# Causal attention: maxima of two heads in the two halves of the array's rows, one burst a step, values two steps behind

## The reference, cut to what matters

```python
Q = (X @ Wq.T + bq).reshape(B, S, H, d_head) * scale
K = (X @ Wk.T + bk).reshape(B, S, H, d_head) * scale
V = (X @ Wv.T + bv).reshape(B, S, H, d_head)
scores = jnp.einsum('bqhd,bkhd->bhqk', Q, K)
causal = jnp.tril(jnp.ones((S, S), bool))
scores = jnp.where(causal[None, None], scores, -jnp.inf)
attn = jax.nn.softmax(scores.astype(jnp.float32), axis=-1).astype(X.dtype)
out = jnp.einsum('bhqk,bkhd->bqhd', attn, V).reshape(B, S, D)
return out @ Wo.T + bo
```

## Time and profile before

| | us |
|---|---|
| median of the runs (3) | 2040.08 |
| lowest, highest | 2039.08, 2040.45 |
| profiled execution, its own time | 2036.14 |
| its span, first to last instruction | 2034.0 |
| TensorE matmuls busy | 1682.5 (83%) |
| VectorE busy | 1383.6 (68%) |
| ScalarE busy | 939.3 (46%) |
| GpSimd busy | 672.0 (33%) |
| mean granted clock of TensorE | 0.923 of 2.4 GHz |

### The profile page before, as it was taken

How to read it: one execution, slowest core, us unless ns; L and a number is a source line. 1 busy time by engine, 2 the same in 40 slices (tenths; PEclk the granted TensorE clock), 3 DMA queues, 4 the chain that set the end, 5 groups by cost and what they waited for, 6 DMA issues and landing times. The chain is left out here.

```text
span 2034.0 us, 35680 instructions
## 1 busy us (share of the span) xinstructions
PE 1682.5 (83%) x10296; PEld 1295.6 (64%) x10296; DVE 1383.6 (68%) x2825; ACT 939.3 (46%) x2201; POOL 672.0 (33%) x850
## 2 busy tenths in 40 slices
PE   2899985709991780799999999996789999979997
PEld 2787774509991560455555555542579999968886
DVE  5688887506665876977777777760467777646776
ACT  0456562304443651066666666664444444433343
POOL 1555530750007824043434334343000000047760
PEclk9799998959995995899999999998899999989999
DMA  6445523723434996333535354422774444466661
GB/s 217 181 141 168 156 47 65 230 91 117 125 113 127 332 355 190 85 105 86 147 85 144 94 129 109 118 68 64 205 216 125 125 126 125 127 212 182 202 181 47
DMA packets 288529, 293.13 MB, mean 144 GB/s; under 512 B 122665, under 2 KB 245034, under 8 KB 286300
## 3 DMA queue, kind: packets, MB, share of 16 engines
q1 hardware_dynamic: 265340, 236.62, 39.6%
q0 software_dynamic: 18432, 50.36, 7.9%
q10 hardware_dynamic: 4608, 4.20, 0.6%
HBM read 144.97 MB, written 141.82 MB: 141 GB/s over the span
## 5 line engine op out<-in xcount | busy, mean ns | idle before, releaser
L1705 ACT ACTIVATE ca_PT<-ca_psS 128x512 f32<-128x512 f32 (+3 forms) x768 | 344.9, 493 | 272.8 <-PE ca_psS L1740 260.4
L1631 DVE TENSOR_REDUCE ca_part<-ca_psM 128x1 f32<-128x512 f32 (+3 forms) x608 | 368.6, 657 | 85.3 <-PE ca_psM L1725 60.5
L1740 PE MATMUL ca_psS<-ca_QS,ca_KS 128*128 128x512 f32 (+3 forms) x768 | 305.7, 408 | 4.2 <-ACT ca_PT L1705 4.1
L1033 POOL DMA_INDIRECT g_y<-ys_scratch,pos x128 | 129.6, 1013 | 441.7 <-POOLq L68 395.0
L1718 PE MATMUL ca_psM<-ca_KS,ca_QS 126*128 126x512 f32 (+3 forms) x768 | 246.5, 364 | 15.6 <-issue 12.8
L1740 PEld LDWEIGHTS ca_psS<-ca_QS,ca_KS 128*128 128x128 f32 x768 | 147.1, 194 | 106.7 <-ACT ca_PT L1705 101.7
L1718 PEld LDWEIGHTS ca_psM<-ca_KS,ca_QS 126*128 126x128 f32 x768 | 141.1, 193 | 37.9 <-DVE ca_part L1631 15.6
L1752 PE MATMUL ca_psO<-ca_PT,ca_VA 128*32 128x512 f32 (+3 forms) x1536 | 160.7, 497 | 1.3 <-POOL ca_PT L1611 1.3
L1609 POOL TENSOR_TENSOR ca_waited<-ca_waited 1x1 f32<-1x1 f32 x128 | 23.4, 183 | 341.7 <-ACT ca_PT L1705 341.7
L626 POOL DMA_INDIRECT xs_scratch<-x_sb,pos x128 | 123.3, 964 | 36.8 <-issue 36.8
L497 PE MATMUL fa_psO<-fa_weighed,ident 128*128 128x256 f32 x512 | 124.0, 398 | 8.1 <-DVE fa_weighed L356 8.0
(11 more groups left out here) (288 smaller groups left out, 4567.2 us busy)
## 6 DMA issues: line engine op xcount, KB each, us to landing
f_xs<-xs_scratch SPq DMA_DIRECT2D x214, 128.0 KB, 2.1
ys_scratch<-f_ys SPq DMA_DIRECT2D x214, 128.0 KB, 1.7
xs_scratch<-fa_blank SPq DMA_DIRECT2D x32, 640.0 KB, 4.1
ca_QS<-qk_scratch SPq DMA_DIRECT2D x32, 512.0 KB, 6.6
ca_KS<-qk_scratch SPq DMA_DIRECT2D x32, 512.0 KB, 8.2
xs_scratch<-fa_blank SPq DMA_DIRECT2D x32, 384.0 KB, 3.4
f_raw<-in_ffn SPq DMA_DIRECT2D x16, 608.0 KB, 4.0
v_scratch<-gp_v_st SPq DMA_DIRECT2D x32, 256.0 KB, 4.5
```

Of the source, the lines that this page charges most:

```text
L1033: pool.indirect_dma_start(dst[:, k, :], None, y_dram, bass.IndirectOffsetOnAxis(pos[:, tile, k:k + 1], 0)).then_inc(got, 16)
L1631: dve.tensor_reduce(dst, psM[(slot * NU + u) % SLOTS][:, 0:nh * w].rearrange("p (h k) -> p h k", h=nh), AX.X, ALU.max)\
L1705: act.activation(PT[:, s % 2, h, off:CHUNK], psS[(GH * s + h) % SLOTS][:, off:CHUNK], ACT.Exp)\
L1740: pe.matmul(psS[tile % SLOTS][:, off:CHUNK], KS[:, slot, h, kt * P:(kt + 1) * P], QS[:, slot, h, c * CHUNK + off:(c + 1) * CHUNK], start=T ...
```

## The change

Six things change in `causal_attention`.

1. The maxima get stacks of their own, `QM` and `KM`: 64 dense rows a head. The first two heads of a group lie in partitions 0 to 63, the other two in 64 to 127. A unit makes its matmuls in pairs, one in each half of the array's rows, into the two banks of a pair (`psM` is now two pairs of banks). The mask is added with two matmuls a unit, which use all rows. VectorE reduces both banks with one instruction. There are 20 units a round and `FIRST` is 8.
2. ORDER becomes "0123uuv": the four scores, then the units, then the values.
3. PT has three slots, and the values are those of two steps before.
4. `psX` goes. The transposes of the output and of the maxima take their turn in the pairs of psM (`place` numbers all users of the pairs in order, with two semaphores, `pair_filled` and `pair_taken`).
5. The transpose of the output of a chunk comes three steps after its last step (`OUT`): in the seventh step for the first chunk, and in the third step of the next round for the second.
6. Two slots instead of three for QS, KS and VA; QM and KM have two of their own, loaded in eight DMAs a round (`pull_pairs`). The last round is written like the others.

```diff
-    SLOTS = 3
+    SLOTS, PAIRS, PTS = 2, GH // 2, 3
...
+        QM, KM = sb("QM", [P, SLOTS, PAIRS, SEQ], F32R), sb("KM", [P, SLOTS, PAIRS, SEQ], F32R)
-        PT = sb("PT", [P, 2, GH, CHUNK])
-        units = [(qt, k0, w, h0, min(CHUNK // w, GH)) for qt in range(POS_TILES)
+        PT = sb("PT", [P, PTS, GH, CHUNK])
+        units = [(qt, k0, w, p0, min(CHUNK // w, PAIRS)) for qt in range(POS_TILES)
                  for k0, w in [(k, min(CHUNK, (qt + 1) * P - k)) for k in range(0, (qt + 1) * P, CHUNK)]
-                 for h0 in range(0, GH, min(CHUNK // w, GH))]
+                 for p0 in range(0, PAIRS, min(CHUNK // w, PAIRS))]
...
-        ORDER = "0u1u2u3uv"
+        ORDER = "0123uuv"
+        OUT = [(s + 3) % NS for s in (max(s for s, (c, _, _) in enumerate(steps) if c == cc) for cc in range(SPAN))]
...
-        psM = [ctx.enter_context(nc.psum_tensor(f"ca_psM{i}", [P, CHUNK], F32)) for i in range(SLOTS)]
-        psS = [ctx.enter_context(nc.psum_tensor(f"ca_psS{i}", [P, CHUNK], F32)) for i in range(SLOTS)]
+        BANKS = 3
+        psM = [ctx.enter_context(nc.psum_tensor(f"ca_psM{i}", [P, 2, CHUNK], F32)) for i in range(2)]
+        psS = [ctx.enter_context(nc.psum_tensor(f"ca_psS{i}", [P, CHUNK], F32)) for i in range(BANKS)]
-        psX = ctx.enter_context(nc.psum_tensor("ca_psX", [P, CHUNK], F32))
...
+            def pull_pairs(n):
+                slot = n % SLOTS
+                if n >= SLOTS:
+                    sp.wait_ge(pair_filled, place["unit", n - SLOTS, NU - 1] + 1)
+                rows = qk_dram[:, :, n, :, :].rearrange("c s (r g h) n -> s g r c (h n)", g=2, h=PAIRS)
+                for g in range(2):
+                    for half in range(2):
+                        part = slice(g * P // 2 + half, (g + 1) * P // 2, 2)
+                        sp.dma_start(QM[part, slot, :, :]...).then_inc(pairs_in[slot], 16)
+                        sp.dma_start(KM[part, slot, :, :]...).then_inc(pairs_in[slot], 16)
...
+            def banks(at):
+                if at >= 2:
+                    pe.wait_ge(pair_taken, at - 1)
+                return psM[at % 2]
-            def unit(n, slot, u):
+            def unit(n, u):
+                pair = banks(place["unit", n, u])
                 for h in range(nh):
-                    ins = pe.matmul(bank[:, h * w:(h + 1) * w], QS[0:STACK, slot, h0 + h, qt * P:(qt + 1) * P],
-                                    KS[0:STACK, slot, h0 + h, k0:k0 + w], start=True, stop=not diag, skip_group_check=True)
+                    for g in range(2):
+                        half = slice(g * P // 2, (g + 1) * P // 2)
+                        ins = pe.matmul(pair[:, g, h * w:(h + 1) * w], QM[half, n % SLOTS, p0 + h, qt * P:(qt + 1) * P],
+                                        KM[half, n % SLOTS, p0 + h, k0:k0 + w], start=True, stop=not diag, skip_group_check=True)
                 if diag:
-                    ins = pe.matmul(bank[:, 0:nh * w]..., ident_b[:, :], mask, start=False, stop=True, ...)
+                    for g in range(2):
+                        ins = pe.matmul(pair[:, g, 0:nh * w]..., ident_b[:, :], mask, start=False, stop=True, ...)
...
                         elif part == "v":
-                            if s:
-                                values(n, slot, s - 1)
+                            if n * NS + s >= PTS - 1:
+                                values(*divmod(n * NS + s - (PTS - 1), NS))
...
-                    if s == last_step[0] + 2:
+                    if s == OUT[1] and n:
+                        transpose_out(n - 1, 1)
+                    if s == OUT[0]:
                         transpose_out(n, 0)
-                    if s == WHOLE - 1:
+                    if s == WHOLE - 1 and n + 1 < ROUNDS:
                         transpose_maxima(n + 1)
-                values(n, slot, NS - 1)
-                transpose_out(n, 1)
```

More of the change, by code:

```diff
@@ L1519, in causal_attention @@
         stack_in = [sem(f"stack_in{i}") for i in range(SLOTS)]
+        pairs_in = [sem(f"pairs_in{i}") for i in range(SLOTS)]
         m_in = [sem(f"m_in{i}") for i in range(SLOTS)]
         ao_stored = [sem("ao_stored0"), sem("ao_stored1")]
[L1522 to L1534, removed]
@@ L1536, in first, with next_place @@
-        def first(n):
-            return isinstance(n, int) and n == 0
+        LOADS, PAIR_LOADS = 5, 8
+        place = {}
+        def next_place(*x):
+            place[x] = len(place)
+        for u in range(NU):
+            next_place("unit", 0, u)
+        next_place("maxima", 0)
+        for u in range(FIRST):
+            next_place("unit", 1, u)
+        for n in range(ROUNDS):
+            for s in range(NS):
+                for u in ahead[s]:
+                    if n + 1 + s // WHOLE < ROUNDS:
+                        next_place("unit", n + 1 + s // WHOLE, u)
+                if s == OUT[1] and n:
+                    next_place("out", n - 1, 1)
+                if s == OUT[0]:
+                    next_place("out", n, 0)
+                if s == WHOLE - 1 and n + 1 < ROUNDS:
+                    next_place("maxima", n + 1)
@@ L1539, in _, with pull @@
+        next_place("out", ROUNDS - 1, 1)
+        masked, slots_done = routing((ctx, block), PT[:, :, :, :].rearrange("p a h n -> p (a h n)"), psO)
         @block.sync
         def _(sp):
[L1541 to L1546, removed]
+            def pull(n):
+                slot = n % SLOTS
+                if n >= SLOTS:
+                    sp.wait_ge(pair_filled, place["out", n - SLOTS, 1] + 1)
+                rows = qk_dram[:, :, n, :, :].rearrange("c s (r h) n -> s r c (h n)", h=GH)
@@ L1574, in _ @@
                              one_rows[:, :].unsqueeze(1).broadcast_to([2, GH * SPAN, CHUNK])).then_inc(ones_done, 16)
+            pull_pairs(SLOTS)
             maxima_rows(0, 0)
-            def beside(n, slot, last=False):
-                if not first(n):
+            for n in range(ROUNDS):
+                if n:
                     output(n - 1, SPAN - 1)
-                if not last:
-                    pull(n + SLOTS - 1, (slot + SLOTS - 1) % SLOTS)
+                if n + 1 < ROUNDS:
+                    pull(n + 1)
                 output(n, 0)
[L1584 to L1588, removed]
+                if n + 1 < ROUNDS:
+                    maxima_rows(n + 1, (n + 1) % SLOTS)
+                if n + 1 + SLOTS < ROUNDS:
+                    pull_pairs(n + 1 + SLOTS)
+            output(ROUNDS - 1, SPAN - 1)
             for c in range(SPAN):
-                output(ROUNDS - 1, c)
                 sp.wait_ge(ao_stored[c], 16 * ROUNDS)
@@ L1691, in back @@
-            def back(n, slot, turn):
-                for c in range(SPAN):
-                    collect(n, c)
-                    divide(n, c)
-            rounds(dve, both, front, back)
+            collect(ROUNDS - 1, 1)
+            divide(ROUNDS - 1, 1)
         @block.scalar
@@ L1748, in values @@
                     pe.wait_ge(exp_done, n * (GH * NS) + GH * s + GH)
-                if kt == 0 and not (first(n) and c == 0):
+                if kt == 0 and (n or c):
                     pe.wait_ge(ot_out, n * SPAN + c)
@@ L1757, in transpose_out @@
             def transpose_out(n, c):
+                pair = banks(place["out", n, c])
                 pe.wait_ge(ot_out, n * SPAN + c + 1)
-                if c == 0:
-                    if not first(n):
-                        pe.wait_ge(o_out, n * SPAN)
-                else:
-                    pe.wait_ge(o_out, n * SPAN + 1)
-                    if not (isinstance(n, int) and n == ROUNDS - 1):
-                        pe.wait_ge(m_neg, n + 2)
-                for q in range(TPC):
-                    ins = pe.transpose(psX[:, q * P:(q + 1) * P], OT[:, q * P:(q + 1) * P], ident[:, :])
@@ new lines, in transpose_out @@
+                ins.then_inc(pair_filled, 1)
+            pe.wait_ge(masked, 2)
+            pe.wait_ge(pairs_in[0], 16 * PAIR_LOADS)
+            for u in range(NU):
+                unit(0, u)
+            transpose_maxima(0)
+            pe.wait_ge(pairs_in[1], 16 * PAIR_LOADS)
+            for u in range(FIRST):
+                unit(1, u)
+            pe.wait_ge(ones_done, 16 * SLOTS)
+            for n in range(ROUNDS):
+                pe.wait_ge(stack_in[n % SLOTS], (n // SLOTS + 1) * (16 * LOADS))
+                pe.wait_ge(m_in[n % SLOTS], (n // SLOTS + 1) * 16)
+                for s in range(NS):
+                    todo = [(n + 1 + s // WHOLE, u) for u in ahead[s] if n + 1 + s // WHOLE < ROUNDS]
+                    if s == WHOLE and n + 2 < ROUNDS:
+                        pe.wait_ge(pairs_in[n % SLOTS], (n // SLOTS + 2) * (16 * PAIR_LOADS))
```

186 lines of the change are left out of this document (83 added, 103 removed).

## The result

| | us |
|---|---|
| before, median of 4 runs | 2040.07 (2039.08 to 2040.45) |
| after, median of 4 runs | 2134.06 (2125.62 to 2142.38) |
| ratio, 95% interval | 1.0463 [1.0427, 1.0499] |
| profiled execution of after, its own time and span | 2125.62 and 2123.9 |
| forecast | 2138, range 2075 to 2185 |

Slower by 94 us. The first lines of the page of after show that the engines have hardly more to do: TensorE is busy for 1724.9 us instead of 1682.5, VectorE and ScalarE for less.

What follows compares the result with a forecast made beforehand. TensorE was taken as the bound, busy 33.8 of a 34.9 us round. Terms +0.4, +6.2, -0.81 and +1.2 made +7.0 a round; with late rounds, ends and lead-in +98 us, so 2138 us, range 2075 to 2185.

Steps and rivals of the forecast that it cites:

- The burst: Steady rounds: with four scores in a row, score 3 waits in every step for score 0's exponential; +6.2 us a round.
- Maxima and masks: Units of a steady round: paired halves save 4.4 us, switches between whole array and halves cost 4.8; +0.4 us a round.
- The loads go side by side: Unit pairs: the two weight loads of a pair were assumed to overlap; in sequence, 2.4 us more a round.
- Rival A: Unit pairs: loads go in sequence (2173 us) or halves don't overlap (2202 us); chance 0.24, as 0.17 and 0.07.
- The copy wait: End of a round: the output transposes' wait for the copy of psO goes; -0.81 us a round.
- The wait for the maxima: Seventh step: TensorE waits 1.5 us instead of 0.29 for VectorE's maxima; +1.2 us a round, bounds 0 and +2.
- The lead-in: Before the steady rounds: taken as bound by VectorE, whose 54 reduces become 28; -3 us, between -0.6 and -6.
- The sum: Whole kernel: 14 rounds at +7.0, +5 for later units and bursts, -2 ends, -3 lead-in; total +98 us.
- the ends: Ends of rounds 14 and 15: they lose the copy wait and part of the wait for GpSimd's cut; -2 us.
- B: Unit blocks: halves cost no switch, -4.8 us a round, 2068 us in all; chance 0.14.
- C: Unit starts and score 3: weight loads run ahead across mode changes and past the waiting score; 2026 us, chance 0.05.
- D: Steady round: no effect if VectorE or ScalarE set its length; called excluded by 26.8 and 21.8 of 34.9 us.

Runs made afterwards that it cites:

- a1: The kernel before with only ORDER changed to "0123uuuuv", four scores in a row, then units, then values; 2143.13 us, ratio 1.0517.
- a2: The changed kernel with ORDER "012u3uv", the first unit of each step between third and fourth score; 2063.17 us, ratio 1.0126.
- b3: The changed kernel with the first maxima's rows ahead of the third load of pairs on SyncE's queue; 2132.11 us, ratio 1.0459.
- c1: b2 with the maxima's matmuls over all 128 rows instead of halves; 2047.09 us, ratio 1.0031.
- b2: The changed kernel with b3's exchange, a step's units between third and fourth score in one visit to the halves, maxima transposed a step later; 2039.73 us, ratio 1.0001.
- a3: The changed kernel with the maxima's matmuls over all 128 rows instead of halves; 2135.84 us, ratio 1.0461.
- b5: b4's kernel again, on an ordinary chip; 2030.55 us, ratio 0.9945.
- d1: The changed kernel with values one step behind instead of two, the copy of psO left in its place; 2320.33 us, ratio 1.1369.
- d3: d2's kernel again, on another chip; 2137.86 us, ratio 1.0485.
- b4: b2 with the output's transposes and division a step later, units spread, mixed units sharing visits, maxima's rows sent before the output; ratio 1.0015 on a slower chip.
- d2: The changed kernel with values one step behind and the copy of psO one step earlier too; ratio 1.0481 on a slower chip.

## Why the prediction was right

**The burst, +6.2 a round: right, and shown.** The four scores take 1.46, 1.23 and 1.01 us, the 512-wide ones 1.67; 1.67, 1.46 and 1.01 were read from the earlier trace rows, and a surcharge of 0.53 was taken for 256 columns. a1 has it without the rest of the change, and a2 takes it out of the change. This term alone comes to 87 us in the 14 intervals, which grew by 88; the others nearly cancel.

**Maxima and masks, +0.4: the sign was wrong, the mechanism right.** The units of a round come to 12.0 us by start to start, 12.6 forecast; for before the prediction's rows gave 12.2. A unit on the diagonal with 512 columns takes 0.76 (1103.44 to 1104.20), forecast 0.80; with 384 columns 0.70, forecast 0.75. A switch in and out costs 0.29, not 0.33: that is the mis-sized term. The price was taken from 128*32 strips and from two-row matmuls, and halves cost a little less. The rule of the Trainium skill (TensorEngine Tiling (Array Packing), Key Properties) that a change of mode drains TensorE agrees with this, and 0.29 for the two is its price here.

**The loads go side by side: right.** Two half-height loads take 0.18 together. By the Trainium skill (TensorE: Matmul & The Clock Gate, LDWEIGHTS) a load costs its columns whatever its rows; the rows above agree, 0.184 for a half load and 0.190 for a whole one, and show that two in different halves don't add up. Rival A is out by it.

**The copy wait, -0.81: right**, no such wait is left. **The wait for the maxima, +1.2: too large.** It became 1.06, so +0.77, because the two reduces of a pair take 1.18 each and the copies 0.24 instead of 0.5. That it would be VectorE's seventh step was right.

These four give -0.2 + 6.2 - 0.81 + 0.77 = +6.0 and the period grew by 6.16 (forecast 7.0); 0.2 is not assigned.

**The lead-in, -3: wrong, it is +5.8.** The step that failed is "the lead-in is bound by VectorE". It was in before. In after VectorE has fewer instructions but TensorE runs at the 1.2 GHz level all through (next section but one), and a third load ahead of the maxima on SyncE's queue made the first score wait 3.10 us. b3 shows the second part, -3.2 us without it, and c1 against b2 the first, as far as it is the halves: 74.3 against 76.6 (in a3, with the load still ahead of the maxima, all rows only make the wait longer, 5.90). With both away the lead-in is where before had it (74.0); that VectorE's fewer reduces gain nothing even then stays open. The prediction had counted the new loads' bytes and not their place in the queue.

**The sum** came out because errors cancelled. The rounds up to the last maxima were forecast at 98 + 5 and came to 88.0 + 5.7; the ends at -2 and came to -3.0; the lead-in at -3 and came to +5.8. That is 98 forecast and 96.5 measured. The 9 us by which the rounds were forecast too long and the 9 us by which the lead-in was forecast too short made each other good. That the total is met to 1.5 us is luck; that the order of the scores makes nearly all of it is not.

**The rivals.** B (halves cost no switch, 2068) is excluded by the 0.44 for a pair and by a3: without switches the halves would have won 4.4 a round over all rows, and they won nothing. C (loads run ahead, 2026) is excluded by the bursts at their full 1.67 and 1.46. D by the result. What C named can be had another way, by not letting the fourth score wait (a2, b2) and keeping the maxima out of VectorE's fullest step (b5), and 2030.55 then lies near its 2026, but it is another sum.

## What to carry to other kernels

Before you put the users of a ring of buffers in a row, count them against the ring: four scores in three banks wait in every step, and in an in-order queue all that stands behind waits too. One other job between the third and the fourth gave back 4.9 of 6.2 us. A mode of the array that packs two matmuls into one paid here only with more than one pair a visit (a visit costs 0.29 us, a 512-wide pair saves 0.23); collect the pairs of a step into one visit before counting the gain. And where a step is moved, look for what stands ahead of its result in the queue of the engine that makes it: in b5 that gave about half of the 0.9 us a round.

## What the runs showed of the hardware that I had not expected

**The clock in the lead-in.** The same stretch of units, by windows of before, after, b2 and c1, each in its own fence in this order (b2's stage starts some 10 us later, so its window does too):

```profile
822.00:832.00 10.00, 7.86 (x27) 5.20 (x27) 9.50 (x13) 0.00 (x0) 0.00 (x0) 0.52 0.01 3
832.00:842.00 10.00, 8.82 (x28) 4.17 (x27) 10.00 (x18) 0.00 (x0) 0.00 (x0) 1.00 0.00 0
```

```profile
832.00:842.00 10.00, 7.94 (x26) 2.86 (x26) 8.88 (x9) 0.00 (x0) 0.00 (x0) 0.50 0.00 0
```

```profile
842.00:852.00 10.00, 8.06 (x28) 3.21 (x28) 8.89 (x9) 0.00 (x0) 0.00 (x0) 0.50 0.00 0
```

```profile
832.00:842.00 10.00, 7.27 (x32) 3.58 (x30) 9.54 (x10) 0.00 (x0) 0.00 (x0) 1.00 0.00 0
```

With halves the granted clock stays at 0.50, the 1.2 GHz level, until the scores come; with all rows, before or c1, it rises to 1.00 long before. The other traces agree: 0.50 with halves (a2, b3, b5), 1.00 with all rows (a1, a3). b2 and c1 differ in nothing but the rows, and c1's lead-in is 2.3 us shorter (74.3 against 76.6). The Trainium skill (TensorE: Matmul & The Clock Gate, What's actually happening) lets the clock follow how busy TensorE has been; here TensorE is shown busy for 0.79 and 0.81 of the window with halves and stays low, and for 0.73 with all rows in c1, at 1.00. So the busy share of a profile does not tell the two apart. What the chip counts there no run here tells. In the steady rounds, between whole-array scores, the halves run at 1.00.

**A wait costs more than its length.** In d1 two waits of 2.91 us a round came with a round 13.5 us longer, and the clock was at the 1.2 GHz level for over ten microseconds behind the one that the windows show. In d3, where the copy is early enough, both are gone: 41.2 us at 1.00.

**Chips differ by 10%.** On one of the chips the kernel before took 2237.51 us instead of 2040. The two traces from there, b4 and d2, have what none of the other twelve has: in the stage ScalarE's exponentials wait 16 times, about once a round, for something that the trace calls remote (another core or an unknown queue), 49.7 us in all and up to 4.4 in b4, 71.3 and up to 6.0 in d2. VectorE's copies wait 30.3 for the same in b4. Behind one such wait, 2.48 us until 979.96, TensorE idles 1.75 and its granted clock is 0.50 from 982 to 990. So b4's rounds were held up, as far as the trace shows, by something other than the kernel's own instructions, and the clock fell behind that. What the remote thing is stays open, and so does whether before's rounds met it as often, as there is no trace of before from that chip.
